# Attention bias added by VectorE in PSUM, weight quantization cut into six pieces, and four rounding steps dropped from the feed-forward quantization

## The reference

```
x = hidden_states                                   # (4, 4096, 2048) f32
h = layernorm(x)
q, k, v = split(h @ Wqkv.T + b)                     # 16 heads of 128
ctx = softmax(q k^T / sqrt(128)) v
x = x + layernorm(ctx @ out_w.T + out_b)
h = layernorm(x)
xq, kq, bq = fake_quant(h, per row), fake_quant(kernel, per column), fake_quant(bias)
y = fake_quant(relu(xq @ kq + bq), per row)
x = x + layernorm(y)
# fake_quant(x): s = max|x| / 127; clip(round(x / s), -127, 127) * s
```

## Time and profile before

| | us |
|---|---|
| median of 2 runs | 7204.73 |
| lowest, highest | 7195.53, 7213.93 |
| the profiled execution | 7194.39 |
| its span on the slowest core | 7192.8 |
| spans of the 8 cores | 7167.1 to 7192.8 |

### The profile page before, as it was taken

One profiled execution on the slowest core, in us unless ns is written; L12 is line 12 of the kernel. 1 busy time (PEld: TensorE's weight loads), 2 busy tenths in 40 slices (PEclk: granted clock), 3 DMA queues, 4 the chain that ended last, 5 costly groups with the idle time before them and its releaser, 6 DMA issues.

```text
span 7192.8 us, 44159 instructions; the slowest of 8 cores (7167.1 to 7192.8 us)
## 1 busy us (share of the span) xinstructions
PE 4096.5 (57%) x16028; PEld 1545.5 (21%) x16028; DVE 2166.9 (30%) x2381; ACT 1290.3 (18%) x1442; POOL 93.5 (1%) x106
## 2 busy tenths in 40 slices
PE   0038999889777777777777777754444303030303
PEld 0013333334222222222222222211111101010101
DVE  4524444211111111111111111122122165756666
ACT  1300000000233333333333333300000000000101
POOL 0000000000000000000000000000000000000000
PEclk9999999999888888888888888966666656565656
DMA  6552212111100000000000000069999910101010
GB/s 167 192 132 59 53 44 61 36 49 45 43 24 24 24 24 24 24 24 24 24 24 24 24 24 24 9 116 163 158 153 162 167 46 27 36 22 41 18 41 24
DMA packets 372461, 431.42 MB, mean 60 GB/s; under 512 B 178967, under 2 KB 334615, under 8 KB 355351
## 3 DMA queue, kind: packets, MB, share of 16 engines
q0 software_dynamic: 137344, 159.40, 15.5%
q1 hardware_dynamic: 193672, 168.17, 8.3%
q10 hardware_dynamic: 41234, 101.02, 3.6%
HBM read 461.77 MB, written 101.01 MB: 78 GB/s over the span
## 4 chain that ended last, share of the span: by engine, by line
PE 40%; DVE 20%; ACT 16%; DMA 14%; issue 4%; DVEq 3%; SPq 2%; ACTq 0%; POOLq 0%
DMA wob<-wo 9%; PE psA L883 8%; PE psB L461 8%; PE psA L892 7%; ACT PT L908 7%; PE psB L626 6%; ACT PT L910 6%; PE psA L1140 3%; PE psA L1407 2%; PE psC L835 2%; DMA xst<-x 1%; PE psD L843 1%; SPq L373 1%; DVEq L532 1%; SPq L1383 1%
## 5 line engine op out<-in xcount | busy, mean ns | idle before, releaser
L461 PE MATMUL psB<-h1fm,wfc 128*128 128x512 bf16 x3072 | 697.7, 389 | 514.6 <-DMA h1fm<-h1h 470.7
L883 PE MATMUL psA<-negCB,onesm 128*128 128x512 bf16 x2048 | 578.5, 408 | 550.1 <-ACT PT L910 288.3
L908 ACT ACTIVATE PT<-psA 128x1024 bf16<-128x1024 f32 x512 | 523.9, 1023 | 1777.6 <-PE psA L892 1777.6
L1400 PE MATMUL psA<-bqB,onesm 128*128 128x512 bf16 x64 | 27.5, 430 | 1089.4 <-DMA xqfm<-xqh 747.4
L892 PE MATMUL psA<-Qh,Kh 128*128 128x512 bf16 x2048 | 604.3, 423 | 0.0
L932 DVE CAST ctxst<-psC 128x512 bf16<-128x512 f32 x64 | 44.0, 687 | 1854.4 <-PE psD L843 1854.4
L835 PE MATMUL psC<-PT,Vh 128*128 128x512 bf16 x2048 | 560.2, 398 | 27.0 <-ACT PT L910 27.0
L843 PE MATMUL psD<-PT,ones_bf 128*1 128x512 bf16 x2048 | 528.1, 380 | 0.0
L910 ACT ACTIVATE PT<-psA 128x1024 bf16<-128x1024 f32 x512 | 521.8, 1019 | 0.0
L461 PEld LDWEIGHTS psB<-h1fm,wfc 128*128 128x128 bf16 x3072 | 303.1, 100 | 905.2 <-issue 570.0
L626 PE MATMUL psB<-wvb,h1fm 128*128 128x512 bf16 x2048 | 470.7, 384 | 0.0
(11 more groups left out here) (165 smaller groups left out, 3125.5 us busy)
## 6 DMA issues: line engine op xcount, KB each, us to landing
wob<-wo POOLq DMA_DIRECT2D x64, 2048.0 KB, 20.9
xst<-x SPq DMA_DIRECT2D x32, 1024.0 KB, 5.8
ktst<-kernT SPq DMA_DIRECT2D x16, 1024.0 KB, 6.2
wfc<-wqk POOLq DMA_DIRECT2D x32, 512.0 KB, 7.6
h1h<-h1t ACTq DMA_DIRECT2D x32, 512.0 KB, 2.8
khh<-kout ACTq DMA_DIRECT2D x16, 1024.0 KB, 8.6
vhh<-vst ACTq DMA_DIRECT2D x128, 128.0 KB, 1.7
Kh<-khh SPq DMA_DIRECT2D x16, 1024.0 KB, 7.3
```

What stands on the lines that cost most here:

```text
L461: ins = nc.tensor.matmul(psB[g % 2][:], wfc[fc % 2][:, dc * 128:(dc + 1) * 128], h1fm[:, dc * 4096 + tt * 512: dc * 4096 + (tt + 1) * 512] ...
L883: nc.tensor.matmul(pa[:, off:off + 512], onesm[:], negCB[:], start=True, stop=False, skip_group_check=True)
L908: nc.scalar.activation(PT[sp][:, 0:1024], psA[0][:], AF.Exp, scale=SMS)
```

## The change

There are three parts. (1) The four bias matmuls of a step are gone; the K and Q matmuls start their slices themselves, and VectorE adds negCB, now F32 and multiplied by 128 when it is copied out of psB, to the four slices in place in PSUM; the exps wait for a new semaphore, `c_badd`. (2) The quantization of a head's weight tile is a queue of six functions, one emitted behind the adds of each step from block 2 on; what is left goes to the head's end. (3) In the feed-forward stage the comparisons with 2.5 and -2.5 are left out, in both quantizations.

```diff
-    negCB = st3.enter_context(nc.sbuf_tensor("negCB", [128, 512], BF16))
+    negCB = st3.enter_context(nc.sbuf_tensor("negCB", [128, 512], F32))
...
+        quantq = deque()
+
+        def _qp1(h=h):
+            wt("vector", d_kn[0], 16 * (h + 1))
+            wt("vector", p3be, p3be.n)
+
+            @on("vector")
+            def _():
+                v = nc.vector
+                v.tensor_mul(kqt[:], kst[0][:], RSKb[:])
+                v.drain()
...
+        def _qp6(h=h):
+            @on("vector")
+            def _(h=h):
+                nc.vector.tensor_mul(kq[:, h * 2048:(h + 1) * 2048], kqa[:],
+                                     SKnb[:]).then_inc(f_kn[0].h, 1)
+            f_kn[0].inc(1)
+        for _p in (_qp1, _qp2, _qp3, _qp4, _qp5, _qp6):
+            quantq.append(_p)
...
-                v.tensor_copy(negCB[:], psB[0][:]).then_inc(c_nr.h, 1)
+                v.tensor_scalar_mul(negCB[:], psB[0][:], 128.0
+                                    ).then_inc(c_nr.h, 1)
...
-                for j in range(4):
-                    @on("tensor")
-                    def _(j=j, hv=hv):
-                        pa, off = hv[j]
-                        nc.tensor.matmul(pa[:, off:off + 512], onesm[:],
-                                         negCB[:], start=True, stop=False,
-                                         skip_group_check=True)
...
-                            start=False, stop=True, skip_group_check=True)
+                            start=True, stop=True, skip_group_check=True)
...
-                wt("scalar", mmS, mmS.n)
+                wt("vector", mmS, mmS.n)
+
+                @on("vector")
+                def _(hv=hv):
+                    v = nc.vector
+                    for pa, off in hv:
+                        v.tensor_add(pa[:, off:off + 512],
+                                     pa[:, off:off + 512], negCB[:])
+                    v.drain().then_inc(c_badd.h, 1)
+                c_badd.inc(1)
+                if qt >= 2 and quantq:
+                    quantq.popleft()()
+
+                wt("scalar", c_badd, c_badd.n)
...
-        wt("vector", d_kn[0], 16 * (h + 1))
-        wt("vector", p3be, p3be.n)
-
-        @on("vector")
-        def _(h=h, par=par):
-            v = nc.vector
-            v.tensor_mul(kqt[:], kst[0][:], RSKb[:])
...
+        while quantq:
+            quantq.popleft()()
...
-                v.scalar_tensor_tensor(qtt[:], qaa[:], 2.5, qtt[:],
-                                       OP.is_ge, OP.add)
-                v.drain()
...
-                v.scalar_tensor_tensor(h2[:], qaa[:], -2.5, h2[:],
-                                       OP.is_lt, OP.add)
-                v.drain()
```

More of the change, by code:

```diff
@@ L1 @@
 import numpy as np
+from collections import deque
 from contextlib import ExitStack
@@ L113, in build_program @@
     fr3 = sem("fr3")
+    c_badd = sem("c_badd")
     fv3 = sem("fv3")
@@ L816, in build_program, with _qp2, _, _qp3 @@
         d_kn[0].inc(16)
+        quantq = deque()
[7 more added lines that the diff above has]
+                v.drain()
+        def _qp2():
+            @on("vector")
+            def _():
+                v = nc.vector
+                v.tensor_copy(kqu[:], kqt[:])
+                v.drain()
+        def _qp3():
+            @on("vector")
+            def _():
+                v = nc.vector
+                v.tensor_sub(kqa[:], kqt[:], kqu[:])
+                v.drain()
+        def _qp4():
+            @on("vector")
+            def _():
+                v = nc.vector
+                v.scalar_tensor_tensor(kqt[:], kqa[:], 0.5, kqu[:],
+                                       OP.is_ge, OP.add)
+                v.drain()
+        def _qp5():
+            @on("vector")
+            def _():
+                v = nc.vector
+                v.scalar_tensor_tensor(kqa[:], kqa[:], -0.5, kqt[:], OP.is_lt,
+                                       OP.subtract)
+                v.drain()
+        def _qp6(h=h):
+            @on("vector")
+            def _(h=h):
[4 more added lines that the diff above has]
+            quantq.append(_p)
         wt("tensor", c_negC, c_negC.n)
@@ L951, in build_program @@
         s_ctx[par].inc(16)
-        wt("vector", d_kn[0], 16 * (h + 1))
-        wt("vector", p3be, p3be.n)
-        @on("vector")
-        def _(h=h, par=par):
-            v = nc.vector
-            v.tensor_mul(kqt[:], kst[0][:], RSKb[:])
-            v.drain()
-            v.tensor_copy(kqu[:], kqt[:])
-            v.drain()
[L963 to L972, removed]
+        while quantq:
+            quantq.popleft()()
     wt("sync", s_den[0], s_den[0].n)
@@ L1458, in _ @@
                 v.scalar_tensor_tensor(zt[:], qaa[:], -1.5, zt[:],
-                                       OP.is_lt, OP.add)
-                v.drain()
-                v.scalar_tensor_tensor(zt[:], qaa[:], -2.5, zt[:],
                                        OP.is_lt, OP.add)
```

## The result

| | before | after |
|---|---|---|
| profiled execution, us | 7194.39 | 7983.92 |
| median of all executions, us | 7396.92 (10) | 8029.11 (11) |
| lowest, us | 7195.53 | 7982.83 |
| after / before | | 1.1115, 95% interval 1.1043 to 1.1187 |
| mean granted clock, slowest core | 0.814 | 0.766 |

A forecast was written before the change was run, and what follows sets the result against it. It took a chain of waits, with no engine full, to bound the kernel. 911 + 251 - 137 - 197 - 151 = +677 us on 7194.39 gave 7871, stated as 7880 us for the median; range 7700 to 8180.

The forecast's parts named there:

- adds, all at the high level: Attention steps: four uncovered PSUM adds replace four bias matmuls, a step going from 4.12 to 5.90 us; +911 us.
- low clock after: Attention after the change: TensorE swings between clock levels, about 45% of steps low; +251 us, bounds 0 and 557.
- low clock before, taken off: Attention before the change: ScalarE's wait beyond the undisturbed waits, put down to low clock stretches; -137 us.
- quantization at 15 heads' starts and the last: Attention: pieces hidden beside the steps save 12.5 us at 15 heads' starts, some 9 at the last; -197 us.
- feed-forward stage: Both feed-forward quantizations: 64 fewer VectorE instructions on the chain, 2.36 us each; -151 us.
- the chain: Attention step: matmuls and exps alternate on single-buffered psA, no engine full; adds lie uncovered between them, making 5.90 us.
- the price of an add: Attention's adds in PSUM: each costs a same-size PSUM copy, 692 ns; four with drain take 2.62 us.
- the clock stays low: Rival for attention: gaps of 3.3 us in each step keep TensorE at the low clock; 8187 us, chance 0.10.
- the forecast's own range: Whole kernel: 7720 to 8060 us, for low shares of 0.15 to 0.75; chance 0.66.
- the end of the range: Whole kernel: upper end, 8180 us, of the stated range from 7700 us, given about 0.8.

The follow-up runs named there:

- quarters: Changed kernel, each step cut into four separately signalled parts (one matmul, one add, one exp of 128x512), adds' drain removed; 6398.0 us, 0.8836 of the kernel before.

## Why the prediction was right or wrong

Each term, against the difference of the two profiled executions:

| term | predicted us | measured us |
|---|---|---|
| adds, all at the high level | +911 | 512 x (5.88 - 4.12) = +901 |
| low clock after | +251 | about +375 |
| low clock before, taken off | -137 | about -147 |
| quantization at 15 heads' starts and the last | -197 | -188 and -7 |
| feed-forward stage | -151 | -146 |
| other stages | 0 | +2 |
| sum | +677 | +790 |

The two clock terms are not measured apart from each other: together they are the +228 us that the other terms leave, and the split is worked out from the distances.

**Right: the chain and the price of an add.** That an add in PSUM costs what a copy out of it does was a choice of the nearest row, and it came out: the add took 692 ns, four took 2.49 us, the step 5.88 to 5.89 us, and the low step 6.72 where 6.75 was worked out. The run without the adds shows that none of it was covered.

**Right: the other two parts.** Their gains came as counted, alone and together, and the run with both of them is faster than the kernel before by the sum. The last of them, 146 for 151, is taken from the first bias matmul of the stage to the end (1400.8 us before, 1255.3 after).

**Wrong: the term of the clock.** The step that failed is the term of 251 us, the one that said that 45% of the steps would be low; about 375 us came. The mechanism, idle time on TensorE that brings the low level to the K and Q matmuls, was right; its size was not. The 45% came from the granted clock averaged over a stage, which was expected at 0.77 and measured at 0.75; that estimate was good. What it was used for was not. The share of time at the low level (about 50%) was taken for the share of steps whose chain is at it. But only four matmuls of a step are on the chain, the first four after TensorE's idle stretch, and that is where the fall comes: (6.481 - 5.88) / 0.85 = 71%, if every low step cost the whole 0.85 us, and 448 x 0.60 = 269 us. The block ends make up the rest of the 375 us: without low clock they would be 9.39 (the short ones before) + 1.76 = 11.15 us from exp to exp, and those from block 0 to 1, from 2 to 3 and to the next head have means of 12.6, 13.5 and 13.4 us. The runs with 12 and with 4 idle-filling matmuls show that the cause is the idle time.

The rival "the clock stays low" put its price at 557 us; the 375 lie between it and the forecast, nearer the forecast. It was wrong as worded: the clock did return in the step shown, too late for the chain, and 101 of 448 distances are those of the high level. The Trainium skill's section "A second HAM failure mode: psum-queue depth-cycling" of the page "TensorE: Matmul & The Clock Gate" says that TensorE, idle for short times between groups of matmuls, swings between the levels; the trace agrees (0.97 in 3018.8 to 3021.2, 0.50 behind it, 1.00 from 3024.6). The advice of that page's table "Why this matters for your kernels" against idle gaps between bursts holds here with 245 us for filling them.

A share of 71% low with the other terms as predicted is 7880 + (0.71 - 0.45) x 557 = 8025 us, against the 8008 of the result; 71% lies inside the shares of 0.15 to 0.75 that the forecast's own range allowed. What lifts 8222 us above the end of the range is the later median of before, and no term of the sum.

## What to carry to other kernels

Work that moves from a full engine to an idle one costs its whole length where it lands in a chain of single-buffered handovers; cut the handover into parts with their own signals first, and only then ask which engine should do the work. Then add up each engine's load again: work that was free beside the chain, as the pieces of quantization were, need not be free beside the cut one. In this kernel the idle gaps between bursts of matmuls cost more than the mean clock said, because the low level met the first matmuls after the gap, which are those that the other engines wait for. Read the clock at the instructions of the chain, not over the stage.

## What was not expected of the hardware

A few matmuls whose result nobody reads made the kernel faster: 4 a step (2048 in all) gave 211 us, 12 a step 245 us. The levels sort most of the steps into two lengths: 357 of 448 are 5.9 or 6.7 us. And VectorE's add in place in PSUM costs the same 692 ns as a copy out of it, whether TensorE and ScalarE work on other parts of psA at that time (quarters: 691 ns) or not (changed kernel: 692 ns).
